# GNN kernel, convolution stage: the edge masks move to GpSimd, and one of four rows of the second norm with them

## The reference, cut to what matters

```python
h = jnp.maximum(_layernorm(x, axis=-1), 0.0)
node = h * deg_isqrt[:, None]
msg  = node[src] * edge_weight[:, None]
N_h  = segment_sum(msg, dst, num_segments=50000) * deg_isqrt[:, None]
out  = (h + N_h) @ W.T + b
x    = x + jnp.where(out >= 0, out, 0.01 * out)
h    = jnp.maximum(_layernorm(x, axis=-1), 0.0)     # the second norm
x    = x + attention_block(h, ...)                  # four attention layers
```

## Time and profile before

| | |
|---|---|
| median of 3 runs | 2285.7 us (2283.72 to 2287.53) |
| the profiled execution: its own time | 2294.79 us |
| the profiled execution: its span | 2293.1 us |
| its mean granted TensorE clock | 0.867 of full speed |
| busy over the whole span: PE, DVE, ACT, POOL | 76%, 70%, 66%, 50% |
| the convolution's steady part | 640 to 820 us of the span |

### The profile page before, as it was taken

One profiled execution on the slowest core, in us unless ns is written; L12 is line 12 of the kernel. 1 busy time (PEld: TensorE's weight loads), 2 busy tenths in 40 slices (PEclk: granted clock), 3 DMA queues, 4 the chain that ended last, 5 costly groups with the idle time before them and its releaser, 6 DMA issues. The chain is left out here.

```text
span 2293.1 us, 41415 instructions
## 1 busy us (share of the span) xinstructions
PE 1745.7 (76%) x9894; PEld 1277.6 (56%) x9894; DVE 1609.0 (70%) x8473; ACT 1513.0 (66%) x7686; POOL 1151.3 (50%) x1069
## 2 busy tenths in 40 slices
PE   2589488888488867866996875996884997884960
PEld 1589355554377764535884544884543885552850
DVE  3671699998599967975555985555995555895860
ACT  0452499999399967963665982665992664993640
POOL 0577777300155538771216772215773224774677
PEclk9995599999599977987996996996995997996985
DMA  7123323221212122212113212113113113123421
GB/s 141 24 51 84 93 78 95 76 64 32 80 51 65 51 64 60 60 46 71 47 47 75 56 42 70 47 47 84 42 46 81 40 45 91 33 51 92 107 70 35
DMA packets 123138, 145.24 MB, mean 63 GB/s; under 512 B 56197, under 2 KB 83637, under 8 KB 122145
## 3 DMA queue, kind: packets, MB, share of 16 engines
q1 hardware_dynamic: 66303, 116.40, 18.6%
q0 software_dynamic: 56160, 25.40, 5.5%
q10 hardware_dynamic: 432, 0.79, 0.1%
HBM read 94.60 MB, written 67.86 MB: 71 GB/s over the span
## 5 line engine op out<-in xcount | busy, mean ns | idle before, releaser
L211 POOL DMA_INDIRECT S<-row_t,rowI x400 | 541.1, 1353 | 232.2 <-issue 232.2
L938 PE MATMUL bank<-AC,XT 128*125 128x390 f32 x800 | 331.6, 521 | 0.4
L1002 ACT ACTIVATE R<-bank 125x128 f32<-125x128 f32 x1200 | 322.8, 305 | 0.0
L1656 POOL TENSOR_TENSOR R<-ident,aselfS 125x250 f32<-125x250 f32 x150 | 90.7, 607 | 391.2 <-PE bank L1684 313.8
L1002 ACT ACTIVATION_READ_ACCUMULATOR R<-bank 125x1 f32 x1200 | 277.1, 239 | 0.0
L1702 PE MATMUL bank<-WCX,XT 128*125 128x130 f32 (+1 forms) x1400 | 250.8, 302 | 0.0
L199 PE MATMUL bank<-ident,Y 125*128 125x125 f32 x800 | 130.8, 289 | 113.4 <-ACT Y L953 58.7
L199 PEld LDWEIGHTS bank<-ident,Y 125*128 125x128 f32 x800 | 98.1, 150 | 213.7 <-issue 139.0
L1789 DVE COPY XT<-bank 128x250 f32<-128x250 f32 x150 | 62.8, 418 | 210.4 <-PE bank L199 210.4
L1702 PEld LDWEIGHTS bank<-WCX,XT 128*125 128x125 f32 x1400 | 182.7, 189 | 43.4 <-issue 1.6
L1044 DVE BATCH_NORM_STATS2 st<-R 125x6 f32<-125x128 f32 x800 | 173.7, 282 | 30.5 <-issue 30.1
(11 more groups left out here) (418 smaller groups left out, 5173.1 us busy)
## 6 DMA issues: line engine op xcount, KB each, us to landing
row_t<-T SPq DMA_DIRECT2D x40, 568.8 KB
R<-in_x SPq DMA_DIRECT2D x100, 224.0 KB
out_rows<-R SPq DMA_DIRECT2D x100, 224.0 KB
R<-m_t SPq DMA_DIRECT2D x5, 2734.4 KB
S<-row_t,rowI POOLq DMA_INDIRECT x400
T<-in_edge_attr SPq DMA_DIRECT2D x1, 5600.0 KB
x_t<-XB SPq DMA_DIRECT2D x50, 112.0 KB
R<-x_t SPq DMA_DIRECT2D x25, 224.0 KB
```

Of the source, the lines that this page charges most:

```text
L211: pool.indirect_dma_start(to, None, table, bass.IndirectOffsetOnAxis(ap=idx, axis=0), bounds_check=rows - 1, oob_is_err=False).then_inc(do ...
L938: nc.tensor.matmul(LAYERS[a][0:P, 0:3 * D + 6], h0(g, a), ACB[:, 0:3 * D + 6], start=True, stop=True).then_inc(layers_done.s, 1)
L1002: ins = nc.scalar.activation(JUNK[:, a * 3 + l, :], LAYERS[a][0:P, l * D:(l + 1) * D], ACT.Square, scale=D ** -0.5, accum_out=NRM[:, g % N ...
```

## The change

Three things change in `conv_layer`. `mask` moves from DVE to POOL, where it comes before `diagonal`. Of the four activations of `normalise2` ACT keeps three; the fourth row (`X1` tile 3 to `T`) is made on POOL by two instructions, `scale_row2` (times the inverse deviation, plus the shift) and `clamp_row2` (the larger of it and 0), the second of which waits for a semaphore of the first. Both stand in POOL's list ahead of `residual`. And two waits are added: PE's `turn2` and POOL's `residual` also wait for the row made on POOL.

```diff
@@ POOL
                         if n >= NS:
                             pool.wait_ge(*rows2.at(n - NS + 1))
+                            pool.wait_ge(*rows2_beside.at(n - NS + 1))
                             pool.wait_ge(*beta_added.at(n - NS + 1))
...
+                    def mask(n):
+                        if n == 0:
+                            pool.wait_ge(s_ml, 32)
+                        if n >= NS:
+                            pool.wait_ge(*gathered.at(n - NS + 1))
+                        nc.gpsimd.tensor_tensor(MA[:, n % NS, :, :], M[:, 2 * n:2 * n + 2, :],
+                                                alphaS[:, 2 * n:2 * n + 2].unsqueeze(2).broadcast_to([P, 2, P]),
+                                                ALU.mult).then_inc(masked.s, 1)
+
+                    def scale_row2(n):
+                        pool.wait_ge(*scaled2.at(n + 1))
+                        r = n % NS
+                        nc.gpsimd.tensor_scalar(T[:, 2 * n + 1, 0:D], X1[:, r, 3, :], rr2[:, r, 3:4], nm2[:, r, 3:4],
+                                                ALU.mult, ALU.add).then_inc(row2_scaled.s, 1)
+
+                    def clamp_row2(n):
+                        pool.wait_ge(*row2_scaled.at(n + 1))
+                        nc.gpsimd.tensor_scalar(T[:, 2 * n + 1, 0:D], T[:, 2 * n + 1, 0:D], 0.0, None,
+                                                ALU.max).then_inc(rows2_beside.s, 1)
+
                     for t in slots:
-                        run_slot(t, NU, [(2, diagonal), (5, residual), (5, add_beta)])
+                        run_slot(t, NU, [(2, mask), (2, diagonal), (6, scale_row2), (6, clamp_row2), (5, residual), (5, add_beta)])
@@ PE
                     def turn2(n):
                         pe.wait_ge(*rows2.at(n + 1))
+                        pe.wait_ge(*rows2_beside.at(n + 1))
@@ ACT, normalise2
-                        for a in range(Q):
+                        for a in range(Q - 1):
@@ DVE: mask is taken out, and
-                        run_slot(t, NU, [(0, statistics1), (8, keep_scores), (6, scale2), (7, copy2), (5, statistics2), (0, aggregate1), (6, edge), (5, aggregate2), (1, invert1), (2, mask), (4, leak), (1, scale1), (5, invert2)])
+                        run_slot(t, NU, [(0, statistics1), (8, keep_scores), (6, scale2), (7, copy2), (5, statistics2), (0, aggregate1), (6, edge), (5, aggregate2), (1, invert1), (4, leak), (1, scale1), (5, invert2)])
```

More of the change, by code:

```diff
@@ L833, in dense @@
              beta_added) = signal(
-                "counted1", "variance1", "root1", "inverse1", "scale1", "rows1_vector", "rows1_scalar", "turned1",
+                "counted1", "variance1", "root1", "inverse1", "scale1", "rows1_beside", "rows1_scalar", "turned1",
                 "turned1_copied", "conv_done", "slope_ready", "leaky_done", "residual_added", "counted2",
-                "variance2", "root2", "inverse2", "scale2", "rows2_vector", "rows2_scalar", "turned2",
+                "variance2", "root2", "inverse2", "scale2", "rows2_beside", "rows2_scalar", "turned2",
                 "turned2_copied", "beta_added")
@@ L1242, in conv_layer @@
                 "rows2_scalar", "turned2", "turned2_copied", "score_ready", "score_kept")
+            rows2_beside, row2_scaled = signal("rows2_beside", "rows1_beside")
             x_stage, x_act, x_pe = signal("crossing_vector", "crossing_scalar", "crossing_tensor")
@@ L1444, in scale @@
                         return op
[L1446 to L1453, removed]
                     def edge(n):
@@ L1516, in conv_layer @@
                         conv_done, sloped, leaked, edged, added, beta_added, counted2, var2, rooted2, inverted2, scaled2,
-                        rows2, turned2, copied2, score_done, score_kept):
+                        rows2, rows2_beside, row2_scaled, turned2, copied2, score_done, score_kept):
                 sig.base += NU
```

## The result

The changed kernel takes 2368.7 us (median of 4 runs, 2366.7 to 2373.0), against 2286.2 for the kernel before beside it: 82.5 us more, a ratio of 1.036 with a 95% interval of 1.034 to 1.038. The forecast was slower, 2331.0 with a range of 2317 to 2356; the time lies above that range.

What follows compares the result with a forecast made beforehand. DVE and ACT together were taken to bound the convolution stage at 4.42 us a slot. A new loop of 5.46 adds 1.04 over 44 distances; with the start, +45.3 gives 2331.0 us, range 2317 to 2356.

Steps and rivals of the forecast that it cites:

- The loop `scale2`, row steps on POOL, `residual`, `statistics2`, next `scale2`: Convolution's steady part: a one-slot loop through DVE and POOL, 5.46 us against 4.42, 1.04 more a slot.
- The floor of 4.37: Loop through ACT and PE (`copy1`, `conv`, `slope`): relieving `normalise2` brings a slot from 4.42 to 4.37, no further.
- the hold of `scale2`: On DVE, 0.28 us of each slot was a wait for POOL's instruction; forecast to be gone as POOL idles then.
- DVE's idle time ahead of `statistics2`: Sign of being right: about 1.1 us idle in each slot, released by POOL's L1284 or by the issue.
- PE at half clock for most of the stage: Named as a sign that the forecast was wrong, in the convolution stage.
- I take 0.35 for the scale ... and 0.30 for the clamp: Estimated lengths in us of POOL's `scale_row2` and `clamp_row2`; the pair was put between 0.40 and 1.00.
- the estimate of about 0.3: From the skill's GPSIMD page, without dispatch: the pair of row steps at about 0.3 us, the slot near 5.1.
- POOL's own slot, 3.93: POOL's old and new instructions added up, 3.93 us a slot, under 4.37: not too full.
- PE is not in the loop: Argument against rival (A): PE lies outside the forecast loop, busy 3.9 of 5.46 us.
- rival (A): More holds of DVE by POOL, a pair at 1.00, or a lower clock: 5.8 to 6.2 a slot, 2345 to 2363; chance 0.18.
- (B): `residual` finds its input early enough, the wait is off the path: slot at the floor 4.37, 2283 us; chance 0.06.
- (C): As (B), but the floor also falls as `conv` is reached sooner; DVE's 4.12 bounds: 2272 us; chance 0.04.

Runs made afterwards that it cites:

- the early bias product: Changed kernel with `residual` and `add_beta` ahead of the row steps, and `conv`'s bias product issued before the wait for `copy1`: 2275.6 us, ratio 0.994.
- the filled kernel: Changed kernel with `turn2`'s four transposes written four times to the same place: 2353.9 us, ratio 1.029 to the kernel before.
- the filling: `turn2`'s transposes written four times: 2353.9 us on the changed kernel, 2371.9 us on the one with only the fourth row moved (`mask` on DVE).

## Why the prediction was wrong, point by point

**Direction and mechanism: right.** The loop `scale2`, row steps on POOL, `residual`, `statistics2`, next `scale2` is there with each of its links, and taking `residual` out of the queue behind the wait takes away the whole loss. The floor of 4.37 under any relief of ACT was right too: it is the slot with `residual` first. `copy2` lies in DVE's wait, the hold of `scale2` is gone, and the added wait of `turn2` is not among the waits of the stage. Two signs were named that came out otherwise. DVE's idle time ahead of `statistics2` was to be about 1.1; the prediction's own terms give about 1.5 (2.29 from `scale2` to `statistics2`, less 0.75 for `scale2` and `copy2`), and it is 1.91. And "PE at half clock for most of the stage" was named as a sign of being wrong: it was, for 60% of the time.

**The size: wrong, and two steps carry it.** The forecast's slot was 5.46, the measured loop is 5.84. Term by term, from the two timelines of one slot after:

| term | forecast | measured |
|---|---|---|
| start of `scale2` to start of `scale_row2` | 0.23 | 0.25 (724.20 to 724.45) |
| `scale_row2` and own wait | 0.43 | 0.53 (to 724.98) |
| `clamp_row2` to start of L1285 | 0.26 | 0.49 (to 725.47) |
| L1285 start to `statistics2` | 1.37 | 1.37 (to 726.84) |
| `statistics2` to next `scale2` | 3.17 | 3.19 (to 730.03) |
| sum | 5.46 | 5.83 |

The failed term is the step "I take 0.35 for the scale ... and 0.30 for the clamp". They last 0.45 and 0.52. The select with one input at 0.28 and the memset at 0.20 were poor neighbours; half of L1291, which stood there as the middle of the bound from above, was no better. Their sum of 0.97 is inside the bounds that were given, 0.40 to 1.00, but at their upper edge, and the estimate of about 0.3 that stood beside it was further off. These two steps are 0.33 of the 0.38 by which the slot was too short; the other terms add 0.05. 0.38 a slot is 16 us over 43 slots, 14 of it from the two steps. They are also why POOL's own slot, 3.93 in the prediction, is 4.17 with the early bias product.

**The clock.** The second step is the sentence "PE is not in the loop", which put the clock into rival (A) alone. At full clock TensorE is not in the loop. The 3.9 us of work that the prediction set against 5.46 is at most 7.8 at half clock, an estimate by doubling, and so over the slot (7.15 was measured); the rows of the ramp had shown a clock of 0.83 with longer slots. Rival (A) had three such slots at 0.4 longer each, and on average over the stage it is 0.36: 15.6 us in the profiled execution, 14.8 in medians by the filled kernel. So rival (A)'s clock was real beside the forecast, not instead of it, and so was its case of a pair at 1.00, 0.35 a slot: the loop of 5.84 is at the lower end of its 5.8 to 6.2. (Its 44 x 1.4 to 1.8 gives 2347 to 2365, not 2345 to 2363.) Its third part, more holds, was not: at full clock `edge` takes 0.17, and in the slots at half clock, where it takes 0.56, DVE waits for TensorE anyway.

Together: 45.3 forecast, 16 for the longer loop, 15.6 for the clock, and some 5 at the two ends of the stage, less 1 for one distance fewer than the 44 counted: 81, as in the profiled executions. At the ends, 0.8 had been counted for the start, and the first two distances cost 2.5: the first (5.49) waited for TensorE at half clock, and in the second the row steps already stood ahead of `residual`. The last four had been put at nothing and cost 3.3. Either of the two errors, the row steps or the clock, would alone have left the time inside the range, at about 2347; both together pass its end of 2356.

**Rivals (B) and (C).** Both are excluded for this order of POOL's list. What they describe is what happens once the order is turned: (B) is the slot of 4.37, and a slot near (C)'s comes with the early bias product.

## What to carry to other kernels

When a step moves to an engine that looks half idle, don't ask whether its slot has room but what the step waits for and what is queued behind it: here 1.0 us of new row work in a list with room for it cost 1.4 us a slot by one position, and nothing in another. Put the step that waits for the newest result last in the slot. Before a slot is made longer, compare TensorE's work for one slot at half clock with the new length, since a stage with more gaps can lose its clock and get a second bound. And read the next loop under a full engine before relieving it: here it allowed 0.05 us of the 0.39 that were taken off, until one product was put ahead of its wait.

## What the runs showed of the hardware

- POOL's instructions with one input are not cheap at 125 x 128: 0.45 us with two columns of factors, 0.52 for a clamp in place with a constant, against 0.64 for a sum of two inputs twice as wide and 0.39 start to start for the activation on ACT that both replaced.
- In slots of 5.84 us the granted clock fell to half again and again. Ahead of L203 TensorE was idle for 1.98 us at 700.24 and again at 706.08, between stretches of work of nearly 4, and the next L203, at 712.76, is at half clock. Shorter idle times came before a fall too: 0.91 at 676.90 and 0.83 at 682.74, where L203 is at half clock. The fall near the start came with a gap of 2.94 (628.98). In the kernel before, with 0.57 idle ahead of the same instruction and slots of 4.42, the clock stayed at 1.00. With the filling it had a mean of 0.96 (0.71 idle in slots of 5.85) and of 0.95 (1.04 idle in slots of 6.17). And at half clock it did not come back at once though TensorE had no gap: from 628.98 to 672 the clock was 0.50 and TensorE was busy all 43 us. What decides between these cases is not shown.
- Some of DVE's small instructions are held to the end of POOL's running instruction: the scale, with two SBUF inputs (`scale2` at 0.42 beside POOL and 0.14 without), and `edge`, a copy within SBUF (0.13 without, up to 0.57 beside POOL). The Trainium skill (SBUF — State Buffer, section "Who interferes with whom") has this as a lock held for the whole instruction, and the trace agrees. Others were not held: the reciprocal L1459 takes 0.14 at 728.31 beside `diagonal`, and `leak`, with one operand in a bank of TensorE's, 0.65 at 728.37, no longer than elsewhere.
